# Last feed-forward of an eight-block layer chain: rank-32 factors laid out four times across the array

## The reference

```python
D_MODEL, D_FF, RANK = (128, 512, 32)
P = jnp.einsum('bsd,dr->bsr', x, U1)
H = jax.nn.gelu(jnp.einsum('bsr,rf->bsf', P, V1) + b1)
Q = jnp.einsum('bsf,fr->bsr', H, U2)
return jnp.einsum('bsr,rd->bsd', Q, V2) + b2
```

## Time and profile before

| | us |
|---|---|
| median of 3 runs | 2283.9 (2283.65 to 2286.96) |
| the profiled execution | 2282.25 |
| its span, first to last instruction | 2280.5 |
| PE busy | 1962.6 (86% of the span) |
| DVE busy | 1336.1 (59%) |
| ACT busy | 1286.9 (56%) |
| mean granted PE clock | 0.916 |

### The profile page before, as it was taken

The page is one execution under the profiler, slowest core; times in us unless marked ns, Lnnn a source line. Parts: engine busy times, 40 slices in busy tenths (PEclk is TensorE's granted clock), DMA queues, the critical chain, the costliest instruction groups (busy, mean ns, idle before and its releaser), DMA issues. The chain is left out here.

```text
span 2280.5 us, 43709 instructions
## 1 busy us (share of the span) xinstructions
PE 1962.6 (86%) x17260; PEld 1378.3 (60%) x17262; DVE 1336.1 (59%) x3330; ACT 1286.9 (56%) x2059; POOL 116.0 (5%) x333
## 2 busy tenths in 40 slices
PE   5799999945855765999999999999994579999997
PEld 3577777723542453777777777777772346666663
DVE  5688888865453524545555454555546567666662
ACT  3699999931324612555555555555562347666662
POOL 3000000000012211000000000000000300000000
PEclk9899999966976867999999999999996779999997
DMA  7211111103224051000000000000000821111110
GB/s 278 91 52 57 54 53 58 39 15 105 100 67 135 8 156 56 1 1 1 1 1 2 1 1 1 1 1 1 1 1 11 258 82 58 55 52 55 58 34 14
DMA packets 60426, 115.12 MB, mean 50 GB/s; under 512 B 7129, under 2 KB 33453, under 8 KB 60225
## 3 DMA queue, kind: packets, MB, share of 16 engines
q1 hardware_dynamic: 57889, 103.62, 14.4%
q0 software_dynamic: 2336, 8.72, 1.1%
HBM read 79.02 MB, written 33.29 MB: 49 GB/s over the span
## 5 line engine op out<-in xcount | busy, mean ns | idle before, releaser
L2597 ACT ACTIVATE a_prT<-bank 128x512 f32<-128x512 f32 (+1 forms) x448 | 232.7, 565 | 328.3 <-PE bank L2506 328.1
L1571 DVE CUSTOM_DVE_ANT_0 a_attn_junk<-wide,a_mask 128x801 f32<-128x801 f32 (+1 forms) x256 | 247.5, 991 | 127.4 <-PE wide L1402 127.2
L1514 ACT ACTIVATE a_attn_prT<-bank 128x512 f32<-128x512 f32 (+1 forms) x448 | 237.0, 566 | 122.1 <-PE bank L1419 109.6
L2622 DVE CUSTOM_DVE_ANT_0 a_sc<-wide,a_zeros 128x1024 f32<-128x1024 f32 (+1 forms) x256 | 243.1, 987 | 91.5 <-PE wide L2492 91.5
L1860 DVE CUSTOM_DVE_ANT_0 a_attn_sc<-wide,a_mask 128x801 f32<-128x801 f32 (+1 forms) x256 | 252.9, 989 | 17.7 <-PE wide L1714 16.0
L1730 PE MATMUL bank<-ident,a_attn_sc 128*128 128x128 f32 x1664 | 244.8, 276 | 15.3 <-ACT a_attn_prT L1819 14.1
L1730 PEld LDWEIGHTS bank<-ident,a_attn_sc 128*128 128x128 f32 x1664 | 198.9, 141 | 62.2 <-issue 42.4
L2506 PE MATMUL bank<-ident,a_sc 128*128 128x128 f32 x1664 | 231.3, 277 | 1.5 <-ACT a_prT L2597 1.5
L2506 PEld LDWEIGHTS bank<-ident,a_sc 128*128 128x128 f32 x1664 | 185.3, 141 | 54.4 <-issue 28.1
L1825 ACT ACTIVATE a_attn_sc<-a_attn_sc,a_attn_nmx 128x1601 f32<-128x1601 f32 x128 | 209.6, 1637 | 8.2 <-DVE a_attn_nmx L1866 8.2
L2492 PE MATMUL wide<-a_kT,a_qT 64*128 64x512 f32 (+1 forms) x1024 | 211.0, 529 | 0.0
(11 more groups left out here) (464 smaller groups left out, 2609.5 us busy)
## 6 DMA issues: line engine op xcount, KB each, us to landing
a_ks<-a_k_parts SPq DMA_DIRECT2D x128, 225.1 KB
a_k_parts<-a_proj_kp SPq DMA_DIRECT2D x24, 416.0 KB, 5.3
a_v_rows<-a_proj_vb SPq DMA_DIRECT2D x8, 936.0 KB, 6.4
a_vs<-a_v_rows SPq DMA_DIRECT2D x32, 234.0 KB
a_q_stack<-a_proj_qp SPq DMA_DIRECT2D x18, 256.0 KB, 3.8
a_qx<-a_q_stack SPq DMA_DIRECT2D x128, 36.0 KB
moe_w1b<-in_e_w SPq DMA_DIRECT2D x15, 256.0 KB, 2.9
ctxT<-in_ctxT SPq DMA_DIRECT2D x4, 832.0 KB, 10.6
```

Of the source, the lines that this page charges most:

```text
L1514: act.activation(prT[0:keys, u % PRT, kt:kt + m, :], bank_of(s, f"W{g}")[0:keys, 0:m * S].rearrange("p (t q) -> p t q", q=S), ACT.Exp).the ...
L1571: dve.tensor_tensor_reduce(junk[:, n % 2, 0:w], S_WIDE[n % 2][:, 0:w], mask(qt, at, w), 1.0, LOWEST, ALU.add, ALU.max, mx[:, p % 2, qt, e, ...
L2597: copy = lambda out, src: act.activation(out, src, ACT.Copy)
L2622: dve.tensor_tensor_reduce(sc[:, s % 2, h, at:at + w], S_WIDE[h][:, 0:w], zeros[:, 0:w], 1.0, LOWEST, ALU.add, ALU.max, mx[:, s % 2, h, p: ...
```

## The change

The three small factors are laid out more than once, and the four chunks take four places in the array:

- u1 is 128x128: its 32 columns stand four times side by side. So p comes out four times, in partitions 0-31, 32-63, 64-95 and 96-127, and `pT` has 128 partitions.
- v1 is stored with chunk i in partitions 32i to 32i+31. The four matmuls of h then use four different groups of 32 rows, and `h_ready` is raised once for each half, on the last. The two halves have banks of their own: 2 to 5, and 6, 7, 0, 1.
- The four matmuls of q use four different groups of 32 columns and write to four groups of partitions of one bank, each complete in itself: the sum over the chunks isn't formed here.
- v2 is stored four times under each other, so that o, now with a contraction over 128 partitions, forms that sum.
- PE does q and o of the first half before q and o of the second; VectorE follows in the same order. The wait for `biased` moves ahead of the copies of q.

The lines of `ffn3_stage` shift by a few; the new numbers are in the rows of the order below.

```diff
-        pT = core.sb(ctx, "ffn3_pT", [RANK, B * S], F32)
+        pT = core.sb(ctx, "ffn3_pT", [P, B * S], F32)
-        qT = core.sb(ctx, "ffn3_qT", [RANK, B * S], F32)
+        qT = core.sb(ctx, "ffn3_qT", [P, B * S], F32)
+        p_bank, h_bank = bank[0:2], (bank[2:6], bank[6:8] + bank[0:2])
+        q_bank, o_bank = bank[2:4], bank[4:6]
+        rows = lambda i: slice(i * RANK, (i + 1) * RANK)
             for c in range(2):
-                pe.matmul(bank[c][0:RANK, :], u1, core.xnT[:, half(c)], start=True, stop=True).then_inc(p_ready, 1)
+                pe.matmul(p_bank[c][:, :], u1, core.xnT[:, half(c)], start=True, stop=True).then_inc(p_ready, 1)
             for c in range(2):
                 pe.wait_ge(p_out, c + 1)
                 for i in range(NC):
-                    if c:
-                        pe.wait_ge(gelu_done, i + 1)
-                    pe.matmul(bank[2 + i][:, :], v1[:, i * P:(i + 1) * P], pT[:, half(c)],
-                              start=True, stop=True).then_inc(h_ready, 1)
+                    ins = pe.matmul(h_bank[c][i][:, :], v1[rows(i), :], pT[rows(i), half(c)], start=True, stop=True)
+                ins.then_inc(h_ready, 1)
             for c in range(2):
                 pe.wait_ge(gelu_done, NC * (c + 1))
                 for i in range(NC):
-                    ins = pe.matmul(bank[c][0:RANK, :], u2[:, i, :], hT[:, c, i, :], start=(i == 0), stop=(i == NC - 1))
+                    ins = pe.matmul(q_bank[c][rows(i), :], u2[:, i, :], hT[:, c, i, :], start=True, stop=True)
                 ins.then_inc(q_ready, 1)
-            for c in range(2):
                 pe.wait_ge(q_out, c + 1)
                 for t in range(4):
-                    ins = pe.matmul(bank[6 + c][:, t * D:(t + 1) * D], qT[:, (4 * c + t) * P:(4 * c + t + 1) * P], v2,
+                    ins = pe.matmul(o_bank[c][:, t * D:(t + 1) * D], qT[:, (4 * c + t) * P:(4 * c + t + 1) * P], v2,
                                     start=True, stop=True)
                 ins.then_inc(o_ready, 1)
...
             for c in range(2):
+                act.wait_ge(h_ready, c + 1)
                 for i in range(NC):
-                    act.wait_ge(h_ready, NC * c + i + 1)
...
+            dve.wait_ge(biased, 1)
             for c in range(2):
                 dve.wait_ge(q_ready, c + 1)
-                dve.tensor_copy(qT[:, half(c)], bank[c][0:RANK, :]).then_inc(q_out, 1)
-            dve.wait_ge(biased, 1)
-            for c in range(2):
+                dve.tensor_copy(qT[:, half(c)], q_bank[c][:, :]).then_inc(q_out, 1)
                 dve.wait_ge(o_ready, c + 1)
...
-            u1, v1, b1 = sb("f3_u1", [P, RANK]), sb("f3_v1", [RANK, FF3]), sb("f3_b1", [P, FF3 // P])
-            u2, v2, b2 = sb("f3_u2", [P, FF3 // P, RANK]), sb("f3_v2", [RANK, D]), sb("f3_b2", [P, D])
+            u1, v1, b1 = sb("f3_u1", [P, P]), sb("f3_v1", [P, P]), sb("f3_b1", [P, FF3 // P])
+            u2, v2, b2 = sb("f3_u2", [P, FF3 // P, RANK]), sb("f3_v2", [P, D]), sb("f3_b2", [P, D])
...
-    a["f3_u1"], a["f3_v1"] = g["L3_ffn_U1"], g["L3_ffn_V1"]
+    a["f3_u1"] = np.tile(g["L3_ffn_U1"], (1, P // RANK))
+    a["f3_v1"] = g["L3_ffn_V1"].reshape(RANK, FF3 // P, P).transpose(1, 0, 2).reshape(P, P)
...
-    a["f3_v2"], a["f3_b2"] = g["L3_ffn_V2"], g["L3_ffn_b2"]
+    a["f3_v2"], a["f3_b2"] = np.tile(g["L3_ffn_V2"], (P // RANK, 1)), g["L3_ffn_b2"]
```

More of the change, by code:

```diff
@@ L1275, in _ @@
             for c in range(2):
+                act.wait_ge(h_ready, c + 1)
                 for i in range(NC):
-                    act.wait_ge(h_ready, NC * c + i + 1)
-                    act.activation(hT[:, c, i, :], bank[2 + i][:, :], ACT.Gelu_apprx_tanh, bias=b1[:, i:i + 1]).then_inc(gelu_done, 1)
+                    act.activation(hT[:, c, i, :], h_bank[c][i][:, :], ACT.Gelu_apprx_tanh, bias=b1[:, i:i + 1]).then_inc(gelu_done, 1)
         @block.vector
@@ L1283, in _ @@
                 dve.wait_ge(p_ready, c + 1)
-                dve.tensor_copy(pT[:, half(c)], bank[c][0:RANK, :]).then_inc(p_out, 1)
+                dve.tensor_copy(pT[:, half(c)], p_bank[c][:, :]).then_inc(p_out, 1)
             dve.tensor_tensor(core.x[:, :, :], core.x[:, :, :], b2.unsqueeze(1).broadcast_to([P, TT, D]), ALU.add).then_inc(biased, 1)
+            dve.wait_ge(biased, 1)
             for c in range(2):
                 dve.wait_ge(q_ready, c + 1)
-                dve.tensor_copy(qT[:, half(c)], bank[c][0:RANK, :]).then_inc(q_out, 1)
-            dve.wait_ge(biased, 1)
-            for c in range(2):
+                dve.tensor_copy(qT[:, half(c)], q_bank[c][:, :]).then_inc(q_out, 1)
                 dve.wait_ge(o_ready, c + 1)
                 dve.tensor_tensor(core.x[:, 4 * c:4 * c + 4, :], core.x[:, 4 * c:4 * c + 4, :],
-                                  bank[6 + c][:, :].rearrange("p (t d) -> p t d", d=D), ALU.add).then_inc(added, 1)
+                                  o_bank[c][:, :].rearrange("p (t d) -> p t d", d=D), ALU.add).then_inc(added, 1)
         @block.sync
```

## The result

| | before | after |
|---|---|---|
| median (6 runs each) | 2283.78 us | 2268.06 us |
| range | 2282.91 to 2286.96 | 2266.29 to 2270.97 |
| ratio, 95% interval | | 0.9934 (0.9924 to 0.9944) |
| profiled execution, span | 2282.25, 2280.5 | 2266.71, 2264.9 |
| first matmul of h to the end of the last add | 25.84 us | 11.28 us |

The kernel is 15.7 us faster by the medians, where 14.7 were forecast (2269.2 against 2268.06).

The account below looks back on a forecast made before the run. TensorE (PE), running h and q on a quarter of the array, was taken to bound the end for 25.84 us; the terms summed to 11.09, 14.7 us less, giving 2283.9 - 14.7 = 2269.2 us, range 2266.8 to 2274.8.

Parts of the forecast that it names:

- The bound, and the stage it rests on: Last stage: PE without a break holds the end, 25.84 us from first h matmul to last add, becoming 11.09.
- p, 128 columns: Matmul p ahead of h: widening from 32 to 128 columns adds about 0.15 us at most, once.
- h, the time of one pair: First half of h: four pairs side by side take one pair's time, 2.14 us until the Gelu.
- Gelus: ScalarE after h's first half: four Gelus 0.57 us apart plus the hand-over to PE, 2.46 us.
- q and o: Tail at clock 1.00: each q 1.09 us, copy 0.74, first o 0.95, second o to the add 1.19.
- Which clock: PE's clock in the last stage: rises in h or at its end, taken as 1.00 from q on.
- The second sum: First h matmul to last add with clock 0.50 throughout: 14.6 us, 11.2 us less than before.
- The first (clock at 0.50): Rival, last stage: clock stays at 0.50 or falls back between h and q; 11.2 us less; chance 0.22.
- The second (side by side only in part, or loads not hidden): Rival, h or q: two row groups at a time, 13.0 us less, or q's loads exposed, 12.9 less; chance 0.10.
- The third: Rival, h and q: row groups run one after another, only columns side by side; 1 to 2 us less; chance 0.03.
- The fourth, an array emptied at each change of group: Rival, h and q: each instruction takes its whole duration, near 33 us against 25.8, +7 us; chance 0.02.

Follow-up runs that it names:

- e9: Changed kernel with h held behind three extra VectorE adds, so PE pauses ahead of h: 15.01 us from h to the last add; 2277.08 us (one run).
- e10: e9 with the four side-by-side matmuls of h's first half issued five times: 16.78 us from h to the last add; 2278.06 us (one run).
- e1: Changed kernel with all four matmuls of h in the same 32 rows: 24.32 us from h to the last add; median 2281.38 us.
- e3: Changed kernel with q accumulated in one group of 32 columns and o on 32 rows: 16.12 us from h to the last add; median 2272.51 us.
- e2: Changed kernel with h one matmul after another, v1 zero-padded to 128 rows: 14.74 us from h to the last add; median 2270.90 us.
- e6: Kernel before, with only u1 laid out four times and v1 zero-padded to 128 rows: 17.41 us from h to the last add; median 2275.45 us.
- e8: Changed kernel with extra identity matmuls at the start of the last layernorm and order q, q, o, o: 9.77 us from h to add; median 2265.79 us.
- e12: The kernel of e8 timed again, beside the changed kernel: 11.39 us from h to the last add; median 2264.62 us.
- e5: Changed kernel with h's four chunks in two groups of 32 rows: 11.87 us from h to the last add; median 2269.20 us.

## Why the prediction was right

- **The bound, and the stage it rests on.** Right. From h to add 25.84 us became 11.28; 11.09 was forecast. The rest of the difference between the two profiled executions, 15.5 us in all, lies nearly all ahead of h (which started 0.90 us earlier, although p took 0.16 us longer), within the scatter that all runs show there. That 11.09 came so close is in part luck: h was 0.14 us shorter than its term, because the clock rose inside it, and the steps from q on were 0.3 us longer.
- **p, 128 columns.** Right: 3.68 us from its start to h instead of 3.52, 0.16 more where at most 0.15 was forecast; the sum, which starts at h, left it out. The copy took 0.69.
- **h, the time of one pair.** Right. To the first Gelu it was 2.00 us; 2.14 was forecast, and the clock's rise in the middle took off the difference. The prediction's bounds were 1.7 and 6.8 us for the matmuls; e9 and e10 put it at the lower one, and e1 shows the upper one. The estimate by the factor of 3.07 in the Trainium skill (TensorE: Matmul & The Clock Gate, section Measured speedup vs the span model), 0.5 us more, was not borne out: at clock 0.50 the first Gelu of e9 came 2.16 us after h, as after one pair alone, and e10 shows the full factor of four.
- **Gelus.** Right: four and the hand-over in 2.47 us (2252.92 to 2255.39), 2.46 forecast; their starts are 0.57 to 0.59 us apart.
- **q and o.** Right within 0.15 us a step: q until its copy 1.21 and 1.14 (1.09 forecast), the copy and the hand-over to PE 0.74, o of the first half 1.09 (0.95), o to the add 1.20 (1.19). The two q and the o between, at + 0.31 in all, are the excess. A part of it is PE's change from o to the next q, an estimated 0.1 us that the sum passed over: the last instruction of o ends at 2258.50, so with a mean of 0.288 it starts at 2258.21, and 0.11 us behind it the q could start, which came at 2258.43. The rest was not traced. q's loads, open by the rule of the Trainium skill (TensorE: Matmul & The Clock Gate, section The mechanism), cost nothing (e3), as L1747 had said.
- **Which clock.** Right in both profiles. The rise came at 2252.5, "in h or at its end", and e10 shows the assumption that had no row: groups of rows count together. But the text gave the clock a share of 3.5 us (14.7 against 11.2) and the layout the rest. e2 and e6 show that the shares depend on the order in which they are taken: padding the rows first, the clock gives 8.4 us to the kernel before, and what is left for side by side and order is 6.1. The second sum was nearly right: e9 measured 15.0 for 14.6, and the 0.4 are o, not h or q. Two things were less sure than the text made them. Work with all rows does not raise the clock by itself: e1 and e9 stayed at 0.50 through 7.9 of 10.4 us of it, and the prediction had q and o at 1.00 only because the rise came in h. And that the clock then outlives the pause before q can't be had from one row of another stage: with that pause e8 kept it and e12 lost it.
- **Rivals.** The first (clock at 0.50) did not occur in either profile of the changed kernel, and would have cost 3.7 us by e9. A fall around a pause does occur: e12 shows one. The second (side by side only in part, or loads not hidden) is excluded by e3, e9 and e10. The third was priced at 1 to 2 us less; e1 made it 1.5. The fourth, an array emptied at each change of group, is excluded by e3 and e9 for both directions. (The items that the prediction gives for its price add up to 36 us; its 33 holds if the 2.5 us of Gelus lie under q, as the new order allows.)

## What to carry to other kernels

Here a matmul with a quarter of the array's rows or columns took as long as a full one, and four of them in different groups took the time of one: with the clock up, 3.5 us for h (e2) and 4.8 for q (e3); look for the rank, head or block dimension that can be laid out four times, and let the next contraction form the sum over the groups. Ask first, though, what the clock is in the stage: PE was busy all the time here and still ran at half speed for 22 us, 14 of them with three quarters of its rows empty; filling these with copies of p against zeros in the weights was worth 8.4 us (e6). And once PE no longer sets the end, order the tail by who is late next, and fill PE's waits ahead of the stage with work that uses all rows.

## What the runs showed of the hardware

- With 32 rows at work, PE busy for 14.00 us of 14.00 left the granted clock at 0.50 (e1); the same columns with 96 rows of zeros added raised it within 2.0 us of h's start (e2), four groups of 32 rows behind a pause within 5.8 us (e10). With 64 rows directly behind p it rose after 1.1 us (e5); whether 64 rows alone would, and whether it does in every run, is open.
- With 128 rows at work but pauses between q and o, 7.94 us busy of 10.40 left the clock at 0.50 (e1; e9 the same with 7.95), where q without a break raised it after 4.3 us.
- At 0.50, four 32-row groups together started a new set of four every 0.85 us, the pace of one group alone (e10).
- At 1.00 the clock outlived 4.37 us busy of 6.80 (changed kernel), but fell after 1.25 us of 4.1 (e12). It did not fall after 1.12 us of 4.05 in another execution of the same program (e8).
- Everything ahead of the last stage varied by up to 10 us between the profiled executions of kernels that are alike up to the last layernorm (the first scaling at 2240.45 us in e2, at 2250.39 in e12). The longer executions mostly show the lower mean granted clock: e12's took 2271.84 us at 0.913, its other four runs 2263.07 to 2264.81 at 0.920 to 0.922. A gain of 1 us in a stage has to be read in that stage.
